# Attention step of a fused transformer layer: another hand-written order of the matmuls of one output block

## The reference

```python
q = x @ Wq + bq
kv = (x @ Wdown + bdown) @ Wup + bup          # k and v of 16 heads, 64 wide
q, k = apply_rope(q), apply_rope(k)           # both at the same t: q.k is unchanged by it
att = softmax(einsum('bthd,btgd->bthg', q, k) / 8, axis=-1)
out = einsum('bthg,btgd->bthd', att, v).reshape(B, T, D)
x = layernorm(x + out @ Wout + bout)
h = silu(x @ wg.T) * (x @ wu.T)               # int weights, divided by 127; hidden 3072
x = layernorm(x + h @ wd.T)
```

## Time and profile before

| | |
|---|---|
| median of three runs | 3531.77 us (3520.87 to 3645.68) |
| the profiled execution | 3540.14 us |
| its slowest core, first to last instruction | 3538.3 us (the eight: 3503.6 to 3538.3) |
| TensorE busy | 77% of the span, 12416 matmuls |
| VectorE busy | 47% |
| ScalarE busy | 23% |
| mean granted TensorE clock | 0.921 on the slowest core |

### The profile page before, as it was taken

One profiled execution on the slowest core, in us unless ns is written; L12 is line 12 of the kernel. 1 busy time (PEld: TensorE's weight loads), 2 busy tenths in 40 slices (PEclk: granted clock), 3 DMA queues, 4 the chain that ended last, 5 costly groups with the idle time before them and its releaser, 6 DMA issues.

```text
span 3538.3 us, 41208 instructions; the slowest of 8 cores (3503.6 to 3538.3 us)
## 1 busy us (share of the span) xinstructions
PE 2714.2 (77%) x12416; PEld 1065.2 (30%) x12416; DVE 1670.1 (47%) x2454; ACT 806.9 (23%) x1363; POOL 292.2 (8%) x540
## 2 busy tenths in 40 slices
PE   0000686889897999789889988898889897989566
PEld 0000222233333333333333333333333333333222
DVE  2221355454455646474646454655465446545312
ACT  0000310141205130523033302431242114221101
POOL 0111000001100110011000100010001000110110
PEclk9999856587999999999999999999999999999778
DMA  6887100211223221412231223222222212232222
GB/s 189 242 241 211 47 1 24 48 42 51 85 69 88 66 87 61 110 54 76 83 110 48 63 93 83 74 62 97 75 86 61 93 63 84 61 95 63 91 76 83
DMA packets 108701, 303.92 MB, mean 86 GB/s; under 512 B 16192, under 2 KB 24768, under 8 KB 108496
## 3 DMA queue, kind: packets, MB, share of 16 engines
q1 hardware_dynamic: 61520, 169.14, 16.3%
q0 software_dynamic: 46976, 132.15, 12.8%
HBM read 269.77 MB, written 39.85 MB: 88 GB/s over the span
## 4 chain that ended last, share of the span: by engine, by line
PE 60%; DMA 10%; DVE 8%; issue 6%; ACT 5%; DVEq 0%; ACTq 0%; POOLq 0%; POOL 0%; SPq 0%
PE P L448 10%; PE P L762 9%; PE P L395 9%; PE P L405 8%; PE P L778 8%; PE P L671 6%; DMA wgb<-wg_s 3%; DMA wub<-wu_s 3%; DVE p_sb L725 3%; PE P L344 2%; PE P L816 2%; DMA wqb<-wq_s 2%; PE P L585 2%; PE P L613 1%; DVE hadb L646 1%
## 5 line engine op out<-in xcount | busy, mean ns | idle before, releaser
L725 DVE TENSOR_TENSOR p_sb<-P,vdup_all 128x512 bf16<-128x512 f32 x1024 | 698.1, 690 | 469.0 <-PE P L778 332.2
L395 PE MATMUL P<-x_bf,wgb 128*128 128x512 bf16 x1536 | 527.4, 404 | 114.4 <-DMA wub<-wu_s 92.9
L405 PE MATMUL P<-x_bf,wub 128*128 128x512 bf16 x1536 | 498.4, 397 | 21.3 <-DVE h_sb L421 21.3
L778 PE MATMUL P<-p_sb,id_sb 128*128 128x256 bf16 x2048 | 494.3, 296 | 25.9 <-DVE p_sb L725 19.4
L448 PE MATMUL P<-h_sb,wdb 128*128 128x512 bf16 x1536 | 498.0, 389 | 13.3 <-DVE r_bf L457 12.3
L646 DVE TENSOR_TENSOR hadb<-q_sb,krep 128x2048 bf16<-128x2048 bf16 x256 | 309.8, 1224 | 347.4 <-PE P L671 260.7
L762 PE MATMUL P<-e_sb,selz_sb 16*128 16x512 bf16 x1024 | 419.2, 418 | 66.0 <-DVE p_sb L725 44.2
L671 PE MATMUL P<-hadb,selred_sb 128*16 128x256 bf16 x2048 | 332.9, 279 | 41.8 <-DVE hadb L646 19.7
L311 PE MATMUL P<-x_bf,wd_sb 128*128 128x512 bf16 x128 | 37.5, 444 | 351.8 <-DMA x_bf<-xt 351.7
L414 ACT ACTIVATE s_sil<-P 128x512 bf16<-128x512 f32 x192 | 114.6, 597 | 719.1 <-PE P L395 718.4
L816 PE MATMUL P<-avn,wob 128*128 128x256 bf16 x1024 | 241.3, 283 | 41.7 <-DMA wob<-wout_s 32.4
(11 more groups left out here) (69 smaller groups left out, 1878.8 us busy)
## 6 DMA issues: line engine op xcount, KB each, us to landing
wdb<-wdn_s SPq DMA_DIRECT2D x64, 768.0 KB, 4.4
wgb<-wg_s POOLq DMA_DIRECT2D x192, 256.0 KB, 3.0
wub<-wu_s POOLq DMA_DIRECT2D x192, 256.0 KB, 3.0
wob<-wout_s SPq DMA_DIRECT2D x128, 256.0 KB, 3.1
wqb<-wq_s SPq DMA_DIRECT2D x64, 256.0 KB, 3.0
yt<-x2b SPq DMA_DIRECT2D x64, 256.0 KB, 2.1
stg<-wg SPq DMA_DIRECT2D x24, 512.0 KB, 5.3
stg<-wu SPq DMA_DIRECT2D x24, 512.0 KB, 5.3
```

The source lines that it names most:

```text
L395: e.matmul(o, l, r, start=st, stop=sp)),
L405: e.matmul(o, l, r, start=st, stop=sp)),
L725: add('V', (lambda e, o=o, a=a, b=b: e.tensor_mul(o, a, b)), waits=w, inc=s_v, d=640)
L778: e.matmul(o, id_sb[:, :], r, start=st, stop=sp)),
```

## The change

Only the order of the 24 matmuls of a block changes, and with it the semaphore values that others wait for. Number and shape of the operations, the buffers and the waits by name (`tt gp-2` and so on) stay.

Before: b0 b1 b2 g0 g1 | b3 g2 g3 | b4 g4 g5 | b5 g6 g7 | b6 g8 g9 | b7 g10 g11 | g12 g13 g14 g15

After: b0 b1 b2 g0 g1 | b3 g2 g3 | b4 b5 g4 g5 g6 g7 | b6 b7 g8 g9 g10 g11 g12 g13 g14 g15

```diff
-                pe_bcast = lambda J, gp: pe0 + J * 24 + (gp + 1 if gp < 3 else 3 * (gp - 1))
-
-                def pe_gsum(J, g):
-                    m = g // 2
-                    return pe0 + J * 24 + (3 * m + 4 + (g % 2) if g < 12 else 21 + (g - 12))
+                AVSCHED = ([('b', 0), ('b', 1), ('b', 2), ('g', 0), ('g', 1),
+                            ('b', 3), ('g', 2), ('g', 3), ('b', 4), ('b', 5),
+                            ('g', 4), ('g', 5), ('g', 6), ('g', 7),
+                            ('b', 6), ('b', 7)] +
+                           [('g', g) for g in range(8, NH)])
+                pos_b, pos_g = {}, {}
+                for k2, (kind2, idx2_) in enumerate(AVSCHED, 1):
+                    (pos_b if kind2 == 'b' else pos_g)[idx2_] = k2
+                pe_bcast = lambda J, gp: pe0 + J * 24 + pos_b[gp]
+                pe_gsum = lambda J, g: pe0 + J * 24 + pos_g[g]
...
-                    sched = [('b', 0), ('b', 1), ('b', 2), ('g', 0), ('g', 1)]
-                    for gp in range(3, 8):
-                        sched += [('b', gp), ('g', 2 * (gp - 2)), ('g', 2 * (gp - 2) + 1)]
-                    sched += [('g', 12), ('g', 13), ('g', 14), ('g', 15)]
                     first = True
-                    for kind, idx2 in sched:
+                    for kind, idx2 in AVSCHED:
```

## The result

The changed kernel takes 3667.64 us (median of 10 runs, 3660.24 to 3715.32), the kernel before 3532.38 (median of 10). The ratio is 1.039, 95% interval 1.037 to 1.042: slower by 3.9%; the medians are 135 us apart. Forecast were 51 us and a range that ends at 3665.

A forecast was written before the change was run, and what follows sets the result against it. TensorE's time plus its waits was taken to bound plan_av's halves beside feed-forward. First supertile 21 lost, series beside feed-forward 39 lost, kept pairs 9 gained: +51 us on 3531.8, 3583 us; range 3506 to 3665.

The forecast's parts named there:

- The direction: Whole kernel: slower by 51 us, 1.4%; chance of slower 0.30, same 0.62, faster 0.08.
- single-block walk: A plan_av block without feed-forward, traced step by step: the next b0 comes at 9.33 instead of 8.02, 1.31 us later.
- First supertile: Its 16 plan_av blocks without feed-forward, at half clock: new waits in series lose 1.3 us each, 21 us.
- 19% of 224: Blocks beside feed-forward: 19% of the new neighbouring b pairs stay together, saving 0.21 us each, 9 us gained (0 to 47).
- The sign I had named: Profile after: runs of b near 7 a block, seen by over 940 of 1024 b weight loads after idle time.
- waits beside feed-forward: The 112 plan_av blocks beside feed-forward: waits in series lose 0.35 us a block, 39 us, between 0 and 90.
- the 120 that I expected: Profile after: TensorE's wait for p_sb in b and g up from 64 us to some 120.
- lower bound of that term: Blocks beside feed-forward: loss of 0, as the planner sees the longer series and moves in more feed-forward matmuls at no cost.
- it had slack: Feed-forward multiplies (L421) behind waiting attention multiplies on VectorE's queue: slack, since VectorE is busy 51 of 77 us.
- The clock was a rival: Halves beside feed-forward: new waits drop the clock, 56 us on top, 3639; chance 0.25, shared with the series not covered.
- Its condition: Clock rival decides when the mean clock of the halves beside feed-forward falls below about 0.95.
- the worst case: All 14 halves beside feed-forward at clock 0.74: 16 us more each, 224 us, 3800.

The follow-up runs named there:

- e13: New order in the first supertile alone, old order in the other seven, against the kernel before: 1.006, 3546 us.
- e6: New order, but in the planner's remaining path each plan_av multiply counts 141 ns less, so a block keeps its old priority; against the kernel before: 1.027, 3615 us.
- e5: Old order, but in the planner's remaining path each plan_av multiply counts 141 ns more, the new order's priority; against the kernel before: 1.025, 3612 us.
- e9: Old order and plan, score reductions of a head put together, and b1, b2 pulled behind the b ahead of them; against the kernel before: 1.011, 3567 us.
- e8: Old order and plan, the eight score reductions (L671) of one head put back to back after planning; against the kernel before: 0.982, 3464 us.
- e7: New order, with the feed-forward multiply (L421) planned first on VectorE within the same 800 ns; against the kernel before: 1.051, 3707 us.
- e10: Old order, with the feed-forward multiply (L421) planned first on VectorE within the same 800 ns; against the kernel before: 1.022, 3602 us.
- e16: New order, with b and the score reductions (L671) both zero-padded to 128x128 weights; against the kernel before: 0.975, 3434 us.
- e11: Changed kernel plus 34 filler matmuls in the first block of half 0 of the seven later supertiles; against the kernel before: 1.034, 3650 us.
- e12: Old order, score reductions of a head put together, plus filler matmuls ahead of each b in the first supertile; against the kernel before: 0.999, 3523 us.
- e14: Old order and plan, b zero-padded from 16x128 to 128x128 weights, same columns and result; against the kernel before: 0.949, 3341 us.
- e15: Old order, with b and the score reductions (L671) both zero-padded to 128x128 weights; against the kernel before: 0.927, 3263 us.
- e3: Planned with the old order, each block's matmuls then executed in the new order within the same slots; against the kernel before: 1.046, 3689 us.

## Why the prediction was wrong, point by point

- **The direction and the single-block walk were right.** First supertile: forecast 21 us, measured 16.6; e13 shows the term alone. From b2 to b2 a block took 9.50 us before and 10.52 after, all but the first two of a half, where the walk has 9.57 and 10.88. What it has too long is mostly the step from a pair of g to their multiply: I took 0.78 us from the first block, and in the others it is 0.71, each time it occurs.

```profile
459.50 1.03 PE L779 MATMUL P<-p_sb,id_sb 128*128 128x256 bf16 x4
460.21 1.29 DVE L730 TENSOR_TENSOR p_sb<-P,vdup_all 128x512 bf16<-128x512 f32 x2 [1.37 <-PE P L779]
```

- **Few pairs stay together.** Forecast was 19% of 224, 9 us. Executed were 43 more pairs beside feed-forward, 19%, and 43 x 0.21 is 9 us. The number held by luck: the loader's row from which I took the 19% doesn't count pairs. Before, 55 of the 224 neighbours there stayed together, 25%, and with the first supertile 87 of 256, not 49. The sign I had named, more than 940 such loads, came true and says nothing.
- **The waits beside feed-forward were sized too small even with the old priority.** Forecast were 39 less 9 us; e6 has 20.3 + 38.1 = 58, inside the bounds of 0 and 90. In all e6 takes some 90 us more than the kernel before on the same chip, not 51. TensorE's waits for `p_sb` rose in the changed kernel from 64 to 113 us, near the 120 that I expected.
- **The step that failed is the lower bound of that term:** "the planner sees the longer series [...] and may put more c into a block [...] this costs nothing by itself". It costs 2.5% by itself (e5), about 90 us, with no wait by name added. I had computed the longer path (8 x 640 + 3 x 564) and used it only as cover. It also decides which of two chains goes first on all five queues, VectorE's as well. There L421 fell behind the softmax, where I had written that it had slack because VectorE was busy 51 of 77 us: an average over the half, which says nothing of the 20 us of the softmax ahead of it.
- **The clock was a rival and should have been a term.** Its condition was met: halves 0 of the slowest core went from 0.95 to 0.85 on average, halves 1 from 0.96 to 0.94, and 3639 was its time. In the profile after cores 4 to 7 spent 687 us at the lower level, before it was 480, so 206 more, 19 of them up to the end of the first supertile's plan_av. If TensorE would have done that work in half the time, the other 187 cost 94 us, most of the 130. It is an estimate, since TensorE doesn't bound every stretch. By the same reckoning e5 has 181 us more, which is 90, as much as all of its loss; e9 has 140 more than e8 (mean of eight cores), 70 of its 97 us of span; and e6 only 23, or 12 of its 77. So by this estimate the priority costs by way of the clock, and the waits in series cost in either way. The half of 93 us at 0.74 in the earlier trace rows, from which I priced the worst case, held some 55 us at 0.812, a level that no core of the changed kernel shows, and was no fair example.
- **Range.** I had a chance of 0.25 for the clock and none for the priority, so the range ended 3 us short.

Open: why e7 and e10 lose with L421 first; what of e16's 170 us is waits and what is placing; and what in the placing lowers the clock, since the gap alone doesn't explain it (e7, e11). That the wide shapes raise the clock is shown, and by what they do so is not: the rows and the shorter time of a b changed together.

## What to carry to other kernels

In a kernel whose order is planned from costs, an edit inside one chain is also an edit of that chain's priority everywhere: compare the planned lists of all engines, and run the old order with the new priority before blaming the edit. Before matmuls are regrouped to save a shape switch, take the switch away with a zero-padded shape of the same columns: here that gave 7.3% where regrouping lost 3.9%. And where TensorE is busy nine tenths of the time beside a chain of waits, a few tenths of a microsecond of new gaps can cost more through the lower clock that follows than by their own length (here some 94 of 130 us, by estimate).

## What the runs showed of the hardware

- The granted clock stayed at 0.50 through a stretch in which TensorE was busy 96 of 103 us (e12, one matmul in four 16x128), and was 0.92 in one in which it was busy 40 of 59 (e14, all matmuls 128x128). I had expected the busy share to decide.
- 512 columns through 16x128 weights or through 128x128 take the same 0.38 us; only the change between them costs, some 0.10 us each way, at weights narrow in rows (b) as in columns (L671; e15 against e14: 2.3% for 527 runs).
- After a gap the lower clock outlasts it by far: 7.2 and 3.1 us without work in the changed kernel were followed by 0.50 until 29 us after the first b (1560 to 1589 us), through 10 us in which TensorE was busy all the time. That the gap alone did it is not shown: e3 and e7 had 0.73 to 0.87 in such halves without it.
